# A gated cross-attention block: the lead-in of its attention loop put in another order

## What is computed

```python
x = x + tanh(g_xattn) * attention(ctx, layernorm(x))
x = x + tanh(g_ffn)  * mixture_of_experts(layernorm(x))

# attention(x=ctx, latents=layernorm(x)), 16 heads of 64:
xn, ln = layernorm(x), layernorm(latents)
q, kv  = ln @ Wq, concat([xn @ Wkv, ln @ Wkv])        # keys and values: 32 context rows, then 512 latent rows
qn, kn = rmsnorm(q) * 64**-0.5, rmsnorm(k)            # per head
out    = softmax(qn @ kn.T) @ v @ Wout + bout

# mixture of experts: softmax router, the best 2 of 8 experts, silu(x @ gate) * (x @ up) @ down
```

## Time and profile before

| what | value |
|---|---|
| median of 3 runs | 366.76 us (366.64 to 366.79) |
| the profiled execution | 366.17 us |
| its span, first to last instruction | 364.4 us, 9315 instructions |
| TensorE busy | 311.2 us (85%) |
| VectorE busy | 287.7 us (79%) |
| GpSimd busy | 255.8 us (70%) |
| ScalarE busy | 194.7 us (53%) |
| mean granted TensorE clock | 0.964 of full speed |
| slot 0's exponential starts | 63.16 us |

### The profile page before, as it was taken

The page is one execution under the profiler, slowest core; times in us unless marked ns, Lnnn a source line. Parts: engine busy times, 40 slices in busy tenths (PEclk is TensorE's granted clock), DMA queues, the critical chain, the costliest instruction groups (busy, mean ns, idle before and its releaser), DMA issues.

```text
span 364.4 us, 9315 instructions
## 1 busy us (share of the span) xinstructions
PE 311.2 (85%) x3618; PEld 192.3 (53%) x3641; DVE 287.7 (79%) x579; ACT 194.7 (53%) x330; POOL 255.8 (70%) x204
## 2 busy tenths in 40 slices
PE   0655676899999999999999999999996999759993
PEld 0332312356555565555565566687874665426562
DVE  3796678688898898888888976945638988889995
ACT  2555444565655656555665645465663436245551
POOL 8698746698888888887987987446862355235652
PEclk9996786899999999999999999999999999999998
DMA  6406101701602504405306239430000000001001
GB/s 174 126 1 153 28 0 24 158 7 24 157 9 54 128 7 95 90 6 127 60 4 153 33 94 202 127 119 3 2 2 0 2 2 0 4 0 31 1 2 30
DMA packets 31470, 20.38 MB, mean 56 GB/s; under 512 B 11650, under 2 KB 30914, under 8 KB 31426
## 3 DMA queue, kind: packets, MB, share of 16 engines
q1 hardware_dynamic: 30482, 19.75, 23.4%
q10 hardware_dynamic: 944, 0.04, 0.2%
HBM read 5.87 MB, written 0.52 MB: 18 GB/s over the span
## 4 chain that ended last, share of the span: by engine, by line
PE 60%; DVE 14%; issue 11%; POOL 8%; ACT 4%; DMA 1%; POOLq 0%; DVEq 0%
PE big L1330 8%; PE big L1331 7%; POOL p_lo L574 7%; PE big L1221 5%; PE o_ps L1196 5%; PE o_ps L1197 5%; PE o_ps L1202 5%; PE tv L1209 4%; PE pj L1173 3%; PE pj L1134 3%; DVE nm_main L877 2%; PE pj L1132 2%; PE tv L1156 1%; PE o_ps L1402 1%; PE tv L1132 1%
## 5 line engine op out<-in xcount | busy, mean ns | idle before, releaser
L546 POOL TENSOR_TENSOR p_lo<-p 128x1024 f16<-128x1024 f32 x64 | 120.7, 1900 | 20.8 <-ACT p L697 20.7
L697 ACT ACTIVATE p<-big 128x1024 f32<-128x1024 f32 x64 | 65.6, 1025 | 57.9 <-PE big L1331 57.9
L877 DVE TENSOR_REDUCE nm_main<-big 128x2 f32<-128x1024 f32 x64 | 78.3, 1223 | 20.5 <-PE big L1221 20.1
L574 POOL TENSOR_TENSOR p_lo<-p,p_lo 128x512 f16<-128x512 f32 x32 | 37.1, 1159 | 47.1 <-ACT p_lo L762 44.8
L452 POOL TENSOR_TENSOR rms_r<-meansq,power 128x8 f32<-128x8 f32 x32 | 52.3, 1638 | 25.3 <-DVE meansq L852 20.9
L1330 PE MATMUL big<-w 128*128 128x512 f16 x128 | 48.7, 381 | 0.8 <-ACT p L697 0.8
L1331 PE MATMUL big<-w 68*128 68x512 f16 x128 | 48.7, 380 | 0.0
L1196 PEld LDWEIGHTS o_ps<-v,p 128*128 128x128 bf16 x512 | 35.6, 99 | 9.2 <-issue 3.9
L1196 PE MATMUL o_ps<-v,p 128*128 128x65 f16 x512 | 40.3, 193 | 0.0
L1197 PE MATMUL o_ps<-v,p 128*128 128x64 f16 x512 | 40.2, 194 | 0.0
L1197 PEld LDWEIGHTS o_ps<-v,p 128*128 128x128 bf16 x512 | 34.1, 97 | 5.4
(11 more groups left out here) (197 smaller groups left out, 744.8 us busy)
## 6 DMA issues: line engine op xcount, KB each, us to landing
w<-hl SPq DMA_DIRECT2D x64, 128.0 KB, 3.5
w<-hl SPq DMA_DIRECT2D x16, 256.0 KB, 3.8
hl<-n_kernel_gating_EDF_dram SPq DMA_DIRECT2D x1, 1024.0 KB, 6.3
hl<-L_ffn_kernel_up_EDF_dram SPq DMA_DIRECT2D x1, 1024.0 KB, 5.6
o_sb<-in_L_xattn_Wkv_dram SPq DMA_DIRECT2D x2, 384.0 KB, 7.0
x_sb<-in_x_dram SPq DMA_DIRECT2D x2, 256.0 KB, 4.4
wout<-in_L_xattn_Wout_dram SPq DMA_DIRECT2D x1, 512.0 KB, 5.2
k1c<-kc_hl SPq DMA_DIRECT2D x32, 8.0 KB, 1.9
```

The costliest lines, as they stand in the source:

```text
L546: nc.gpsimd.tensor_tensor(p_lo[m % NP][:, :], p[m % NP][:, :], p_hi[m % NP], ALU.subtract).then_inc(plo_ok, 1)
L574: nc.gpsimd.tensor_tensor(hid_lo[m % NH], hid[m % NH], hid_hi[m % NH], ALU.subtract).then_inc(hlo_ok, 1)
L697: nc.scalar.activation(p[n % NP][:, :], st_ps, ACT.Exp).then_inc(exp_ok, 1)
L877: nc.vector.tensor_reduce(nm_main[:, u % 2, 2 * c:2 * c + 2, q], s2_ps.rearrange("p (k n) -> p k n", k=2), AX_X, ALU.max, negate=True).the ...
```

## The change

The second unit's tiles no longer take all four banks of `big`: tiles 4 to 7 pass through its first two banks, and the scores and maxima of unit 0 go on in the other two as soon as unit 0's own tiles are turned. TensorE, VectorE, ScalarE and GpSimd have their lead-in lists woven anew. The context's squares and scaling stand later on VectorE, its key power later on GpSimd. The projection of tile 8 moves from slot -4 to just before it, the four first values move to the slots -4 to -1, all through o_ps[1]. The steps on the second entry's variance and scale move from GpSimd to VectorE, in slots -2 and 1, with only the two powers left on GpSimd (the first in the lead-in, the second in slot 0); what hangs on them moves four to five slots later (z from -1 to 2, its turning from 1 to 5). Three semaphores are new. In the diff, the marks between the maxima on VectorE stand for the context's squares (kc_sq, kc_ms), the scaling of the context's keys and their low half (`cklo_ok`), in this order, and the one in its slot for the low half of the context's values (`cvlo_ok`); on TensorE they stand for the turning of the context's keys (`ckT_ok`) and the context's values (`cv_mm`).

```diff
@@ slots
-        LN1_AT = -3
+        LN1_AT = 2
+        V1_AT = {FIRST + t: t for t in range(QT)}
...
         def qk_bank(tau):
-            return big[:, 512 * (tau % QT):512 * (tau % QT + 1)] if tau < 2 * QT else pj[:, :]
+            k = tau if tau < QT else tau % 2
+            return big[:, 512 * k:512 * (k + 1)] if tau < 2 * QT else pj[:, :]
-        def first_v_bank(t):
-            return (pj, tv)[t % 2][:, :]
@@ gpsimd, behind inverse_rms(3)
-            pool.wait_ge(cms_ok, 1)
-            nc.gpsimd.tensor_tensor(kc_r[:, :], kc_ms[:, :], power[0:BC, :], ALU.pow).then_inc(crr_ok, 1)
-            for tau in range(QT, 2 * QT):
-                inverse_rms(tau)
-            for i in range(NG + 1, W_ALL):
-                weights_lo(i)
+            rsqrt(CH_B1A)
             nc.gpsimd.memset(K2c[1][:, :], 0.0).then_inc(const_z, 1)
...
+            inverse_rms(4)
+            inverse_rms(5)
+            weights_lo(NG + 1)
+            weights_lo(NG + 2)
+            pool.wait_ge(cms_ok, 1)
+            nc.gpsimd.tensor_tensor(kc_r[:, :], kc_ms[:, :], power[0:BC, :], ALU.pow).then_inc(crr_ok, 1)
+            copied_lo(0)
+            inverse_rms(6)
+            copied_lo(1)
+            inverse_rms(7)
+            for i in range(NG + 3, W_ALL - 1):
+                weights_lo(i)
+            copied_lo(2)
+            copied_lo(3)
+            weights_lo(W_ALL - 1)
@@ gpsimd, slot(n)
-                if n == LN1_AT:
-                    second_entry_norm()
-                if n == LN1_AT + 2:
+                if n == -1:
                     one_hot(1)
+                if n - 1 in V1_AT:
+                    t = V1_AT[n - 1]
+                    pool.wait_ge(vf32_ok, t + 1)
+                    nc.gpsimd.tensor_tensor(V[0][:, t, :, DH + 1:VW], ...)
+                if n == LN1_AT - 2:
+                    pool.wait_ge(ln1v_ok, 1)
+                    nc.gpsimd.tensor_tensor(ln_t[:, CH_B1B, 2, :], ln_v[:, CH_B1B, :], power[:, 0:QT],
+                                            ALU.pow).then_inc(ln1p_ok, 1)
@@ scalar, slot(n)
-                if n == LN1_AT + 2:
-                    act.wait_ge(ln1_step, 7)
+                if n == LN1_AT:
+                    act.wait_ge(ln1b_ok, 1)
                     for t in range(QT, T):
...
+                if n in V1_AT:
+                    t = V1_AT[n]
+                    act.wait_ge(v_mm, t + 1)
...
@@ vector, behind low_halves(3)
+            maximum(0)
+            normalise_qk(4)
+            maximum(1)
+            normalise_qk(5)
...
+            maximum(2)
+            mean_squares(6)
+            maximum(3)
+            mean_squares(7)
+            maximum(4)
...
+            maximum(5)
+            normalise_qk(6)
+            maximum(6)
+            normalise_qk(7)
...
+            maximum(7)
+            def second_entry_variance():
+                r, t = ln_r[:, CH_B1A, :], ln_t[:, CH_B1B, :, :]
+                dve.wait_ge(lnr_ok, CH_B1A + 1)
+                link(nc.vector.tensor_tensor(t[:, 0, :], r, r, ALU.mult))
+                link(nc.vector.tensor_tensor(t[:, 1, :], t[:, 0, :], moments[:, QT:T, 1], ALU.mult))
+                nc.vector.tensor_scalar(ln_v[:, CH_B1B, :], t[:, 1, :], LN_EPS, None, ALU.add).then_inc(ln1v_ok, 1)
+            def second_entry_scale():
+                t, tok = ln_t[:, CH_B1B, :, :], slice(QT, T)
+                dve.wait_ge(ln1p_ok, 1)
+                link(nc.vector.tensor_tensor(ln_s[:, tok], ln_r[:, CH_B1A, :], t[:, 2, :], ALU.mult))
+                link(nc.vector.tensor_tensor(t[:, 0, :], moments[:, tok, 0], ln_s[:, tok], ALU.mult))
+                nc.vector.tensor_scalar(ln_b[:, :], t[:, 0, :], -1.0, None, ALU.mult).then_inc(ln1b_ok, 1)
@@ vector, slot(n), behind mean_squares
+                if n == FIRST + 2:
+                    second_entry_variance()
+                if n == FIRST + 1:
...
+                if n == LN1_AT - 1:
+                    second_entry_scale()
@@ tensor, behind turn_tile(3)
+            score(0)
+            score(1)
+            for tau in (4, 5):
+                pe.wait_ge(lo_ok, tau - 1)
+                turn_tile(tau)
+                project_tile(tau + 2, qk_bank(tau + 2), 0, 2 * GC).then_inc(qk_mm, 1)
+                score(tau - 2)
+            score(4)
+            score(5)
...
             for tau in (6, 7):
                 pe.wait_ge(f32_ok, tau - 5)
                 turn_tile(tau)
+                score(tau)
+            pe.wait_ge(wlo_ok, W_ALL - 1)
+            project_tile(2 * QT, qk_bank(2 * QT), 0, 2 * GC).then_inc(qk_mm, 1)
...
@@ tensor, slot(n)
-                if n == LN1_AT + 4:
+                if n == LN1_AT + 3:
                     need_tv(pe, n)
                     turn_rows(1, tv)
...
+                if n in V1_AT:
+                    first_values(V1_AT[n])
```

More of the change, by code:

```diff
@@ L500, in _, with copied_lo @@
             last.then_inc(const_z, 1)
-            for t in range(QT):
+            def copied_lo(t):
                 toks = slice(t * P, (t + 1) * P)
@@ L516, in _ @@
             pool_step = [0]
[L518 to L529, removed]
             def second_scale(b):
@@ L644, in _ @@
             high_halves(3)
+            high_halves(4)
             squared(6)
+            high_halves(5)
             squared(7)
@@ L655, in _ @@
             high_halves(7)
[L656 to L664, removed]
             def evacuate(i):
@@ L732, in slot @@
                                    ).then_inc(nmc_ok, 1)
+                if n in V1_AT:
+                    t = V1_AT[n]
+                    act.wait_ge(v_mm, t + 1)
+                    nc.scalar.activation(V[0][:, t, :, 0:DH], o_ps[1][:, :].rearrange("p (h d) -> p h d", d=DH), ACT.Copy,
+                                         scale=V_SCALE).then_inc(vhi_ok, 1)
+                    need(act, vlop_ok, t - 1)
+                    nc.scalar.activation(copies[2 + t % 2], o_ps[1][:, :], ACT.Copy, scale=V_SCALE).then_inc(vf32_ok, 1)
                 if n in TURN_AT:
@@ L1227, in first_values @@
             def first_values(t):
-                project(first_v_bank(t), slice(t * P, (t + 1) * P), (0, 2)).then_inc(v_mm, 1)
+                if t == 0:
+                    pe.wait_ge(wlo_ok, W_ALL - 2)
+                    pe.wait_ge(f32_ok, QT)
+                need(pe, vf32_ok, t)
+                project(o_ps[1][:, :], slice(t * P, (t + 1) * P), (0, 2)).then_inc(v_mm, 1)
             pe.wait_ge(wlo_ok, 1)
@@ L1258, in _ @@
             last.then_inc(ckT_ok, 1)
-            for tau in (4, 5):
-                pe.wait_ge(lo_ok, tau - 1)
-                turn_tile(tau)
             for tau in (6, 7):
@@ L1264, in _ @@
                 turn_tile(tau)
-            pe.wait_ge(norm_ok, 2 * QT)
-            for j in range(8):
-                score(j)
-                if j == 0:
-                    pe.wait_ge(wlo_ok, W_ALL - 2)
-                    for g in range(NG):
-                        last = project(st_ps[:, g * GC:(g + 1) * GC], ctx_rows, slice(g * W3 + 2 * GC, (g + 1) * W3))
-                    last.then_inc(cv_mm, 1)
-                if j in (2, 3, 4, 5):
-                    t = j - 2
-                    if t == 1:
-                        pe.wait_ge(cklo_ok, 1)
-                    need(pe, vf32_ok, t - 1)
-                    first_values(t)
+                score(tau)
+            pe.wait_ge(wlo_ok, W_ALL - 1)
+            project_tile(2 * QT, qk_bank(2 * QT), 0, 2 * GC).then_inc(qk_mm, 1)
+            for g in range(NG):
+                last = project(st_ps[:, g * GC:(g + 1) * GC], ctx_rows, slice(g * W3 + 2 * GC, (g + 1) * W3))
+            last.then_inc(cv_mm, 1)
             def times_values(m):
```

60 lines of the change are left out of this document (24 added, 36 removed).

## The result

| | before | changed |
|---|---|---|
| median of 20 runs | 366.57 us | 367.8 us |
| the profiled execution | 366.17 us | 367.35 us |
| its span | 364.4 us | 365.5 us |

The ratio of the changed kernel to the one before is 1.0031, with a 95% interval of 1.0015 to 1.0046: it is slower by 1.1 us (0.6 to 1.7). The forecast was 368.3 on a median of 366.76, that is +1.5 (a sum of +1.6, rounded down). In the experiments one execution of e5, its profiled one, took 458 us at a granted clock of 0.66; it is left out of the ratio and nothing is read from its trace.

What follows compares the result with a forecast made beforehand. TensorE bounds the kernel from 80 us on, so the lead-in sets the change's price: -2.7 (start to tile 9) + 0.6 (GpSimd) + 3.1 (VectorE held) + 0.6 (rows turned) = +1.6, forecast 368.3 us; 8-in-10 range 364.8 to 370.2.

Steps and rivals of the forecast that it cites:

- Up to slot -4: Lead-in up to slot -4's context scores: they start at 51.5 us, 2.9 us earlier than 54.37.
- Slot -4 to tile 9: Context scores to tile 9's mean squares: 8.4 us, ending at 59.9, 2.7 us earlier than before.
- GpSimd behind tile 9: GpSimd's longer list up to tile 10's power: 8.95 us against 8.34, +0.6 us.
- The held steps: Slot 1: VectorE's three scale steps wait for GpSimd's p_lo 0, p_lo 1 and pc_lo, +3.1 us.
- Rows turned in slot 5: Turning the second entry's rows in TensorE's bound stretch instead of slot 1: +0.6 us, bounds 0.4 and 0.66.
- Sum: Whole kernel: -2.7 + 0.6 + 3.1 + 0.6 = +1.6 us, 368.3 us on the median of 366.76.
- (a): Slot 1: small steps not held, or GpSimd idle; -1.4 to -1.6 us, 365.2 us; chance 0.25.
- (b): Slot 1: only one of the three steps held to the end; +0.3 to +0.7 us, 367.2 us; chance 0.12.
- (c): Lead-in: TensorE falls to half clock among scores and maxima and stays; +3.7 us, 370.4 us; chance 0.11 with (e).
- (d): Beside tile 9's power: powers hold VectorE too, delaying the variance's steps; +2.9 us, 369.6 us; chance 0.05.
- (e): Lead-in: new order brings nothing, another wait replaces that for key transfers; same as (c), chance 0.11 together.

Runs made afterwards that it cites:

- e5: Kernel of e1 plus four TensorE transposes in slot 1 whose result nobody reads; ratio to the kernel before 0.9948, run again 0.9988.
- e1: Changed kernel with the second entry's three scale steps on VectorE ahead of tile 10's scaling in slot 1; ratio to the kernel before 0.9986.
- e2: Changed kernel with only the lead-in order: second entry's variance and scale back on GpSimd, its turning in slot 1; ratio to the kernel before 0.9903.
- e7: Kernel of e2 with the second entry's rows turned in slot 5 instead of slot 1; ratio to the kernel before 0.9955.
- e9: Kernel of e7 plus four transposes in slot 1 whose result nobody reads; ratio to the kernel before 0.9928.
- e3: Changed kernel with GpSimd's one-hot rows for unit 1 written in the lead-in, not in slot -1; ratio to the kernel before 0.9983.
- e4: Changed kernel with the three scale steps at the same place, each reading at most one operand from SBUF, others in PSUM; ratio to before 0.9969.
- e6: Edits of e2 and e3 together on the changed kernel; ratio to the kernel before 0.9873, run again 0.9872.

## Why the prediction was right

**Up to slot -4.** Forecast 51.5, measured 52.32, inside the bounds of 50.6 and 52.9. The list of VectorE ended at 45.80 + 0.68 = 46.48, between the 46.0 taken and the 46.8 of half clock: the clock was 0.66 from 28 to 38 and half throughout from 40 to 52 (0.51), where I had taken a mean of either level. The stretched issue, which I had left out, came again (1.30 for 0.6).

**Slot -4 to tile 9.** Forecast 8.4 us, measured 59.82 - 52.32 = 7.5, under my full-clock value of 7.9: TensorE was at full clock here. The two errors, +0.8 and -0.9, nearly cancel, and tile 9 is 2.79 us earlier than before, 2.7 forecast. That is partly luck. In e1, whose instructions are the same up to there, TensorE ran part of the stretch at half clock and it took 8.4 us. Over the profiled executions of the kernels with this lead-in order, slot 0's scores start anywhere from 58.6 to 61.2; e2, e7 and e9 have the same instructions up to there and start it at 60.02, 61.20 and 58.61.

**GpSimd behind tile 9.** Forecast +0.6, measured: 68.80 - 59.82 = 8.98 against 8.34, +0.6. e3 confirms it, by taking 1.7 of it away.

**The held steps.** Forecast +3.1, measured from tile 10's power to tile 11's mean squares 76.17 - 68.80 = 7.37 against 4.76, +2.6. The mechanism was right: e4 takes the steps' waits away at the same place, e1 at another. The size was 0.5 too large: I had the three end 5.2 us after the power, 0.4 beyond the 3.75 + 1.04 of GpSimd's backlog, but they ended 4.73 after it, with pc_lo itself. What I missed is the limit behind them: TensorE at half clock after its wait for tile 10. It cost e1 0.45 us and e4 1.7 of their stretches, and nothing that can be seen in the changed kernel, where VectorE was later still.

**Rows turned in slot 5.** Forecast +0.6; e9 against e2 shows 0.5, and slot 6's scores show it in the changed kernel (tile 11 is turned 0.5 later than before, slot 6 starts 1.0 later).

**Sum.** -2.8 + 0.6 + 2.6 + 0.5 = +0.9 against the +1.1 of the spans and of the ratio; the forecast was +1.6, and the difference is mostly the 0.5 of the held steps. Held against e2, which has the same lead-in order and reached slot 0 at the same time (60.02 and 59.95), what the moved steps cost from slot 0 to slot 6 is 25.49 - 21.53 = 3.96 us: 0.80 up to tile 10's turn (GpSimd's longer list), 2.64 for the held steps (the stretch against e5 again), 0.52 for the rows in slot 5. The rivals: (a), steps not held, and (b), only one of them held, are refuted by the three rows at 69.43 to 72.56; the time of (a) is what e4 gives (0.9969 of 366.57 is 365.4, where (a) had 365.2), though e4 has other losses. (c), half clock, happened in its first half only. (d) falls by L944 and L945, 0.20 and 0.17 us inside tile 9's power. The row at 17.34 that I held against it is a scaling with one tensor input, as is the one of 0.71 beside pc_lo, and says nothing of products with two; the products inside a power are L944 here and L951 and L952 in e1. (e), the order brings nothing, falls by e2.

## What to carry to other kernels

Before small steps go from one engine to another, look at what runs beside their new place: three VectorE operations of 0.2 us took 4 us of VectorE beside a GpSimd backlog, and 0.2 us each when they stood about 2 us earlier, beside a power, or read PSUM. When a stage is woven anew, keep the parts of the change apart: here the new order was worth 3.6 us (3.0 by the spans) and the moved steps hid it. An operation that looks free to move may be what keeps TensorE's clock up, so its old place has a price as well as its new one.

## What the runs showed of the hardware

**What holds a small VectorE operation.** Products with two SBUF inputs and a scaling from SBUF to SBUF waited for GpSimd's subtractions in both kernels that had these three steps beside them, the changed one and e3 (1.23, 1.82 and 0.97 us for 0.2); with one input in PSUM they didn't (e4: 0.15 to 0.17). The Trainium skill gives the cause on the page SBUF — State Buffer, section Who interferes with whom: the second read port of VectorE is GpSimd's. The trace agrees for the two products beside subtractions. GpSimd's power operation reads SBUF as well, and held nothing: products of 0.20 (L944), 0.14 and 0.16 us (L951 and L952 in e1) in its 1.64 us. There the measurement goes against the page's general sentence. Whether a power reads SBUF only in a small part of its time, no run here shows. The scaling has one tensor input, so the second port as such doesn't explain it; the runs show only that it was held when it read SBUF and not when it read PSUM.

**One lead-in, several times.** Among the kernels with this lead-in order slot 0 started between 58.6 and 61.2 us, and between 59.2 and 61.0 in two executions of one kernel, e6. Two parts can be told apart. Up to the context scores' start, the executions without fill in the lead-in differ by 1.7 us (50.98 to 52.69). From there to slot 0 they fall on two values: 7.63 or 7.64 us in the changed kernel, e2, e4, e5 again, e6 and e9, with a granted clock of 0.99 to 1.00 from 52 to 63, and 8.51 to 8.55 in e1, e3, e6 again and e7, with 0.84. TensorE waits for the key transfers ahead of it; the first six had waited 0.15 to 1.23 us and went on at full clock, the other four 1.44 to 1.94 us and fell to half clock soon behind the wait. So half clock there costs 0.9 us, and one trace is not enough to size a term of this lead-in.

**The clock across a wait.** After a wait of 1.84 us TensorE turned tile 10 at half clock in e1 (1.09) and at full clock in e5 (0.63), which had four more transposes ahead of the wait; after 1.01 us it was 1.02 in e7, and 0.63 in e2 and e9, which had four transposes in slot 1. Here the length of the wait alone doesn't tell the level; what ran before it counts as well. How long the half clock lasts differs too, about 2 us in e1 and 5 in e4. Each of these is one execution.
